# Token-row sends of an attention stage: eight in each of the last three batches instead of four in each of the last six

## The reference, cut to what matters

```python
# for each of 8 sequences: q, k, v, norm, rotary, window attention, output projection
logits = jnp.clip(xt @ gate_w.T, -50.0, 50.0)
top_w, top_idx = jax.lax.top_k(logits, 2)              # two experts for each token
rw = jax.nn.softmax(top_w, axis=-1)
deltas = jax.nn.softmax(expert_atom_weights, axis=-1) @ atoms
weighted = deltas * jax.nn.sigmoid(importance)         # [8 experts, 4096]
rows, cols = mask_idx // H, mask_idx % H               # 4096 cells of a 512x512 matrix
vals = jnp.einsum('tk,tks->ts', rw, weighted[top_idx])
contrib = jax.ops.segment_sum((xt[:, cols] * vals).T, rows, num_segments=H)
out = xt @ W.T + contrib.T
```

## Time and profile before

| | |
|---|---|
| median of 3 runs (lowest, highest) | 1020.61 us (1020.23, 1024.21) |
| profiled execution, whole | 1018.18 us |
| its span in the trace | 1016.4 us |
| mean granted TensorE clock | 0.964 of full speed |
| PE busy | 950.8 us (94%) |
| DVE busy | 562.7 us (55%) |
| ACT busy | 399.3 us (39%) |
| POOL busy | 361.1 us (36%) |
| cell scatters, POOL L636 | 32, 52.1 us busy, 158.5 to 294.6 us |
| sends of both layers, POOL L628 | 64, 64.7 us busy |

### The profile page before, as it was taken

How to read it: one execution, slowest core, us unless ns; L and a number is a source line. 1 busy time by engine, 2 the same in 40 slices (tenths; PEclk the granted TensorE clock), 3 DMA queues, 4 the chain that set the end, 5 groups by cost and what they waited for, 6 DMA issues and landing times.

```text
span 1016.4 us, 18703 instructions
## 1 busy us (share of the span) xinstructions
PE 950.8 (94%) x4754; PEld 619.8 (61%) x4755; DVE 562.7 (55%) x2431; ACT 399.3 (39%) x1256; POOL 361.1 (36%) x475
## 2 busy tenths in 40 slices
PE   8999899998959998859999999999999999999997
PEld 3457465655635555524444447888767767767764
DVE  5777768886749789753333432556733333333332
ACT  3653357655636566201111111222524344334332
POOL 3576016576763260303433430333312221211212
PEclk9995799999989999979999999999999999999999
DMA  7864924345335364359888746994745445545431
GB/s 258 265 244 122 339 62 111 90 117 130 68 97 175 105 204 155 115 179 221 195 200 196 176 100 212 347 392 168 226 93 119 103 94 113 116 85 110 99 72 37
DMA packets 82065, 160.35 MB, mean 158 GB/s; under 512 B 17479, under 2 KB 22743, under 8 KB 80464
## 3 DMA queue, kind: packets, MB, share of 16 engines
q1 hardware_dynamic: 45712, 95.39, 29.0%
q0 software_dynamic: 24832, 42.71, 20.3%
q10 hardware_dynamic: 11456, 21.51, 6.7%
HBM read 102.17 MB, written 69.00 MB: 168 GB/s over the span
## 4 chain that ended last, share of the span: by engine, by line
PE 50%; DMA 19%; DVE 10%; issue 9%; POOL 8%; DVEq 3%; SPq 1%; ACT 0%; POOLq 0%; ACTq 0%
PE ps L725 41%; DMA acc<-R,tok_i 11%; DMA m_buf<-tot,cell_i 5%; PE ps L731 3%; POOL m_buf L636 3%; DVE R L1675 2%; DMA R<-m_buf 1%; DVE R L1657 1%; PE ps L799 1%; DVEq L2027 1%; DMA R<-rows 1%; PE ps L780 1%; POOL R L622 1%; POOL R L598 1%; POOL R L607 1%
## 5 line engine op out<-in xcount | busy, mean ns | idle before, releaser
L725 PE MATMUL ps<-R 128*128 128x128 f32 (+4 forms) x2768 | 677.9, 400 | 11.1 <-DVE R L2026 3.6
L725 PEld LDWEIGHTS ps<-R 128*128 128x128 f32 x2768 | 416.2, 192 | 222.0 <-issue 202.2
L699 POOL DMA_INDIRECT out_x<-R,tok_i x39 | 60.6, 1554 | 229.0 <-DVEq L2115 138.1
L1319 ACT ACTIVATE R<-ps,inv_f 128x128 f32<-128x128 f32 x156 | 44.5, 368 | 175.7 <-PE ps L725 167.0
L628 POOL DMA_INDIRECT rows<-R,slot_i x64 | 64.7, 1011 | 131.8 <-ACT lg L1283 62.4
L699 POOL DMA_INDIRECT acc<-R,tok_i x39 | 60.6, 1555 | 118.6 <-DVE R L2026 115.4
L731 PE MATMUL ps<-ident,R 128*128 128x128 f32 x440 | 67.7, 285 | 25.2 <-DVE R L1675 10.1
L731 PEld LDWEIGHTS ps<-ident,R 128*128 128x128 f32 x440 | 53.8, 146 | 53.8 <-issue 34.6
L1141 ACT ACTIVATE R<-R,nmx 128x384 f32<-128x384 f32 x128 | 78.0, 615 | 18.2 <-DVE nmx L1646 15.8
L1646 DVE CUSTOM_DVE_ANT_0 R<-ps,R,q_scale 128x384 f32<-128x384 f32 x128 | 76.1, 614 | 9.9 <-issue 9.9
L1311 ACT ACTIVATE R<-R 128x2048 f32 x39 | 74.6, 1913 | 2.2 <-issue 2.0
(11 more groups left out here) (330 smaller groups left out, 977.4 us busy)
## 6 DMA issues: line engine op xcount, KB each, us to landing
R<-rows SPq DMA_DIRECT2D x78, 258.0 KB, 5.6
R<-in_b SPq DMA_DIRECT2D x39, 256.0 KB
m_buf<-R SPq DMA_DIRECT2D x8, 1024.0 KB, 13.5
R<-m_buf SPq DMA_DIRECT2D x16, 512.0 KB, 4.3
R<-in_fc ACTq DMA_DIRECT2D x16, 512.0 KB
R<-acc SPq DMA_DIRECT2D x32, 256.0 KB
R<-in_fc ACTq DMA_DIRECT2D x8, 1024.0 KB
R<-in_x_t SPq DMA_DIRECT2D x4, 1024.0 KB, 9.1
```

The lines of the kernel that those rows point to most:

```text
L699: po.indirect_dma_start(out=sums[s], out_offset=bass.IndirectOffsetOnAxis(ap=tok_i[:, s:s + 1], axis=0), in_=rows[s], in_offset=None, boun ...
L725: m = pe.matmul(out, lhs(k), rhs(k), start=(k == 0 and first), stop=(k == KC - 1 and last))
```

## The change

POOL's loop no longer issues sends with b = 2, 3 and 4. The 24 sends of tiles 0 to 11 stand at the end of the iterations b = 5, 6 and 7, eight in each: tiles 0 to 3, 4 to 7 and 8 to 11. The wait for `r_slot` is put ahead of each second tile as it was. No other engine's instructions change, and no send is added or dropped.

```diff
                     scales(b + 1)
                 next_cells()
                 for n in range(4):
-                    if b >= 2:
-                        if n == 0:
-                            po.wait_ge(S["r_slot"], b - 1)
-                        send(a_rows, 2 * b - 4 + n // 2, n % 2, S["xs_sc"])
                     next_cells()
+                for t in range(4 * (b - 5), 4 * (b - 4)) if b >= 5 else ():
+                    if t % 2 == 0:
+                        po.wait_ge(S["r_slot"], t // 2 + 1)
+                    for c in range(2):
+                        send(a_rows, t, c, S["xs_sc"])
             po.wait_ge(S["zdone"], 16 * 11)
```

## The result

| | before | after | |
|---|---|---|---|
| median (lowest, highest) | 1020.69 us (1020.23, 1024.21), 4 runs | 1037.24 us (1033.83, 1043.34), 4 runs | ratio 1.0168, 95% interval 1.0138 to 1.0197 |
| profiled execution, whole | 1018.18 us | 1043.34 us | |
| its span; mean granted clock | 1016.4 us; 0.964 | 1041.6 us; 0.944 | |

The forecast was 1020.0 us with a range of 1016.5 to 1024.0. The change is slower by 16.6 us, outside the range. The profiled execution of the kernel after is the slowest of its four runs, and its span is 25.2 us longer than that of before: sizes read from this pair are larger than the difference of the medians.

The account below looks back on a forecast made before the run. The prediction took POOL's chain of cell scatters and the fetch of piece 0 before DVE's first addition as the bound. Terms -0.8 + 0.2 + 0 = -0.6 us, from a median of 1020.61, gave 1020.0 us, range 1016.5 to 1024.0.

Parts of the forecast that it names:

- Scatters between sends: POOL's scatters of b = 2 and 3: removing eight sends between them costs +0.2 us, ends -1.1 and +2.3.
- The fetch of piece 0: `m_buf` fetch before DVE's first addition: without four sends beside it, 0.8 us gained, ends nothing and 1.3 us.
- The estimate by the Trainium skill's fixed cost: Same first `m_buf` fetch, from fixed completion cost and queue turns: 3.6 us, a term of 1.5 us instead of 0.8.
- Twelve sends come to b = 5, 6 and 7: Late batches: POOL's idle time covers the added sends and `m_buf` fetches have 4 us to spare; term 0.
- The slower rival: PE's pauses at starts of batches 5 and 6: added sends prolong them and lower the clock, 1024.0 us; chance 0.14.
- point of decision: PE's pauses between batches: the slower case decides once they reach 4 us in place of about 2.
- signs of being wrong: Scatters under 3 us apart, last before 290 us, 5 us fetch, PE pauses over 3 us, clock 0.50, late DVE wait.

Follow-up runs that it names:

- e3: Kernel after with its 24 sends split four, four and sixteen over b = 5, 6 and 7; 1041.57 us, ratio 1.0186 to before.
- e2: Kernel after with SP's copies to `acc` moved to the first four batches; 1041.34 us, ratio 1.0201 to before.
- e8: Kernel before, each send from b = 5 on waiting until the one before has landed; 1015.96 us, ratio 0.9962 to before.
- e16: Kernel after, sends of b = 5 and 6 replaced by eight each with 64-byte rows, all 24 full sends in b = 7; 1060.1 us.
- e1: Kernel after, each of the 24 sends waiting until the one before has landed; 1029.36 us, ratio 1.0059 to before.
- e5: Kernel after with 64 waits for a long-set semaphore ahead of the batches in ACT's program; 1037.5 us, ratio 1.018 to before.
- e17: Kernel after, b = 5 and 6 sending eight full-row sends each to another tensor, spaced by small POOL operations, 24 real sends in b = 7; 1032.74 us.
- e14: e10's kernel unchanged, on chip C; 1029.67 us, ratio 1.0086 to before.
- e15: Kernel after, b = 5 and 6 with eight plain 264 KB transfers each on SP's queue, 24 sends in b = 7, chip C; 1044.95 us.
- e10: Kernel after, b = 5 and 6 with eight plain 264 KB transfers each on POOL's queue, 24 sends in b = 7, chip B; 1009.88 us.
- e4: Kernel after, sends of b = 5 and 6 replaced by eight quarter-row sends each, all 24 full sends in b = 7, chip A; 1059.3 us.
- e13: e4's kernel unchanged, on chip C; 1060.01 us, ratio 1.0384 to before.
- e12: Kernel after, unchanged, on chip C; 1039.20 us, ratio 1.0183 to before.
- e7: Kernel after, sends of b = 5 and 6 begun only behind the second masking of the next batch; 1030.55 us, ratio 1.0086 to before.

## Why the prediction was wrong

*Scatters between sends, +0.2 us.* Right within its ends. The interval of 3.38 us that I took was measured again (3.38 and 3.37), and the five scatters of b = 3 took 273.99 - 260.44 = 13.55 us, 0.3 more than before. Those of b = 2, which I had counted at nothing, took 234.58 - 220.11 = 14.47 us instead of 13.41, the end that I had given for them, by one interval of 4.41 us. The last scatter came 3.03 us later, but 1.9 us of that is the whole chain's later start: the first was at 160.43 instead of 158.52, ahead of anything the change touches. The stretch from first to last went from 136.1 to 137.2 us, 1.1 us more, inside the ends of -1.1 and +2.3. One pair of traces can't tell this from chance: the same stretch takes 134.9 to 137.8 us in thirteen of the fifteen other traces without sends between the scatters (139.9 in e3, 140.8 in e2, where copies run beside it) and 135.7 to 136.8 us in the four with them.

*The fetch of piece 0, -0.8 us.* Right: 5.10 to 4.29. It holds in every trace: from the issue to DVE's start it is 3.96 to 4.42 us in the 16 without sends beside the fetch, and 5.12 to 5.51 us in the four with sends. The estimate by the Trainium skill's fixed cost ("DMA: Bandwidth & Descriptors", anatomy of one DMA) and turns of the queues (the same page, queues, rings and completion order) was 3.6 us; the measured times decide against it. The page states the fixed cost for DMAs issued from GpSimd, and this fetch is SP's.

*Twelve sends come to b = 5, 6 and 7: 0.* This is the step that failed. What it says of POOL is right, POOL had idle time to spare, and no later wait of DVE for a piece of `m_buf` grew by over 0.2 us. But it counted only POOL and the fetches as those that sends can touch. A row of sends holds up PE, which shares neither queue nor semaphore with them. The term put at 0 measured 21.5 us in the profiled pair: 17.1 us of pauses and 6.6 us of longer busy time at the lower clock, less 2.2 us of other idle time. The medians lie 16.6 us apart.

*The slower rival.* It had this mechanism: the pauses of the earlier trace rows were put down to sends in flight, and e8 shows that they were, 2.24 to 0.73 us. It had 0.14 and 2.7 + 1.3 us, and was mis-sized: I priced a second group of four like the first, while eight in a row at the first boundary and sixteen at the second cost 6.3 and 7.8 us more than four, and the clock stayed at half for longer. Its point of decision, pauses of 4 us, was passed twice over, and pauses over 3 us were among my signs of being wrong. I held against it that the first four sends stood there already, and that a queue served in turn need not hold longer because more waits behind. The first was evidence for it, and the second reasons about the DMA queues, in which the cause doesn't lie as far as bytes go: e16 moves next to nothing.

**Shown:** that rows of sends close to each other make the pauses (e1 against e5 on chip A, e17 against e16 on D), that it is not the traffic, the bytes, the copies to `acc` or POOL's queue (e2, e14, e15, e16), and that PE is the engine that is late (the semaphores' times). **Argued, with one difference left in each:** that it is the indirect form (POOL is also done sooner with eight plain transfers), and that it depends on the chip (e10 against e14, one run on B). **Open:** through what a row of indirect sends reaches PE, and what is different on chip B. The Trainium skill ("DMA: Bandwidth & Descriptors", SWDGE vs HWDGE vs iDMA) says that GpSimd writes the descriptors of its DMAs into rings in SBUF, and names DVE as the engine that this can collide with. DVE's operations kept their durations here (100.13 us busy against 100.29 in the stretch above), and plain transfers from POOL, by that page built in the same way, did no harm; so the page's mechanism alone doesn't explain it. The kernel after was not run on chip B; that it would be level with before there is an inference from e10. Why e4 had a short first pause on chip A and e13 a long one on C isn't known either.

## What to carry to other kernels

Idle time of the issuing engine is no cover for a row of indirect DMAs: look at what PE does beside the rows that are there already, and price a longer row by more than its share. Space them, by a wait for the one before or by other work between them (2.5 us apart did no harm here), and leave them in the batches where a scatter's flight spaces them for nothing: there eight sends cost the chain of scatters nothing that the change could give back. Where an idle time of PE is put down to "issue" and those of DVE and ACT to "remote", compare the end of PE's last row with the time at which its semaphore went up. And time a change on more than one chip before taking its size for the kernel's.

## What the runs showed of the hardware

- Indirect sends of 128 rows, issued 1.3 us apart, delay PE's completions by up to 7.8 us in the first row of eight (the kernel after, e12, e13; 2.4 in e4), by 12.1 to 15.4 us in a row of 24 (e14, e15, e17) and by 21.9 to 23.9 us in a row of 32 (e4, e13, e16), against the ends that their rows state; with rows of 64 bytes (5.5 us and a pause of 7.86, e16) as with rows of 2064 bytes. In the kernels before and after no completion of DVE or ACT is late by over 0.02 us between 320 and 430 us. PE's late completions come in steps: 343.39 and 346.25 us in the kernel after, and in e7 355.63, 358.51 and 361.38 us, 2.9 us apart.
- The traces from one chip of four don't show it: PE busy 17.52 of 20 us there and 7.63 on another, with the same kernel, sends and traffic. The kernel before is 5 us faster on that chip (1015.93 us), as fast as its paced version is on chip A (1015.96 us).
- Eight plain transfers of 264 KB from POOL's queue take POOL 4.50 us to issue (0.56 each), eight indirect ones 10 us (e12), and only the second hold PE up.
- Fetches of 512 KB on SP's queue beside a row of 24 sends took 5.9 to 9.2 us to land in e10, against 3.8 to 5.1 us in the kernel before.
